# Attention scores of a half row: both bank waits ahead of the first of two matmuls

## The chip, the cores and the metric

The kernel runs on one core of one Trainium2 chip. The metric is the device time of one execution in microseconds (us); lower is better.

## The reference, cut to what matters

Three blocks follow each other: cross attention of 4 x 128 queries to 4 x 2048 keys with 16 heads and a bias, a gated recurrence with ternary weights and its gated MLP, and a mixture of 8 experts. The change touches the first alone:

```python
h = NUM_HEADS                       # 16, each 32 wide
q = _split_heads(query_antecedent @ Wq, h) * d_head ** (-0.5)
k = _split_heads(memory_antecedent @ Wk, h)
v = _split_heads(memory_antecedent @ Wv, h)
logits = jnp.einsum('bhqd,bhkd->bhqk', q, k) + bias
weights = jax.nn.softmax(logits, axis=-1)
x = jnp.einsum('bhqk,bhkd->bhqd', weights, v)
b, _, l, d = x.shape
x = x.transpose(0, 2, 1, 3).reshape(b, l, h * d)
return x @ Wo
```

with 4 batches, 128 queries and 2048 keys. The two blocks behind it are the gated recurrence (its state goes through a scan) and `_moe` with the best 2 of 8 experts.

## The kernel before, in words

Everything of the attention is written out by hand: each engine has one program in order, and the engines meet in counted semaphores. `pe`, `dve`, `act` are TensorE, VectorE, ScalarE. `x.made(key)` counts a semaphore up when an instruction is done, and `wait_ge(*x.at(key))` waits for that count.

A batch `b` has four quads of four heads each; quad `n` has the place `g = n % 4` in its batch. A row `j` of a quad is one head: 128 queries by 2048 keys. It is scored in four chunks `c` of 512 keys, one matmul each (L482), and each chunk fills one of the three PSUM banks of the ring `scores`. VectorE takes a chunk out of its bank, adds the bias, keeps a running maximum (`add_bias`, L712, followed by the instruction that reads the accumulator), and so counts `biased` and sets the bank free. ScalarE takes the exponential of a whole row (L894). TensorE turns the weights over through the identity (`turn_pair`, 8 transposes of two key tiles, L502), ScalarE (L902) or VectorE (L722) moves them out, and TensorE multiplies them with the values (`multiply_pair`, L517, 16 matmuls of 32 columns for a pair, the weights loaded as 128x32 tiles). The quad's sums are turned at L527 (`turn_sums`), copied by VectorE at L738, and the quad is closed by VectorE at L746 (`finish`), which waits for the quad's last product.

The order of TensorE around the change: a quad has eight slots, two for a row. Slot `i` scores half a row, that is two chunks, and then turns a pair of key tiles of the quad before; in every second slot it also multiplies two pairs. In the first quad of a batch (`g = 0`), and in two slots of the second, projections of values and keys (L429 to L431, L412 to L414) stand in place of the turning. When the fourth quad has been scored, a tail without scores turns and multiplies what is left (`TAIL`), and the projections of the next batch follow. Between a batch's scores and the next batch's lie some 90 us of projections.

With three banks and two chunks a slot, chunk number k of a batch's sequence waits until VectorE is done with chunk k-3. The first chunk of a slot thus waits for a bank that has long been free or nearly so, the second for a bank that VectorE frees one chunk later. After quads with `turn_sums` the sums take a turn of the ring too, so that for one chunk `sums_copied` stands in place of `biased`.

The waits of a matmul are carried out ahead of its weight load. The diff touches `score` (removed) and `score_slot`.

Of the kernel before, what the change touches and what calls it, by code (L numbers as in the profile page):

```python
# [27 lines left out]
CHUNK = 512  # L28
# [105 lines left out]
def perceiver_block(nc, a, out):  # L134
    with ExitStack() as life:
        def sb(name, shape, dt, stack=life):
            return stack.enter_context(nc.sbuf_tensor(name, shape, dt))
# [4 lines left out]
        def events(name, keys, by=1):  # L142
            return Events(sem(name), list(keys), by)

        psum = life.enter_context(nc.psum_tensor("psum", [P, 8, BANK], F32))
# [16 lines left out]
        def scalars(name):  # L162
# [31 lines left out]
        qstack = sb("qstack", [P, 2, QUAD, P], F32R, region_r)  # L194
# [8 lines left out]
        wq_sb, wk_sb, wv_sb, _, x_in, q_all, q_hi, q_lo = (view(s) for s in range(8))  # L203
# [19 lines left out]
        queries_in = [events(f"queries{i}_in", [n for n in quads if n % 2 == i], 16)  # L223
                      for i in range(2)]
# [9 lines left out]
        def in_ring(n, j):  # L234
            return n % DT >= 2 or n % DT == 1 and j == 0

        def ring_turn(n, j):
            return QUAD * (n % DT - 2) + j + 1 if n % DT >= 2 else 0
# [14 lines left out]
        def stack_in(n, j):  # L253
            return ring_in[ring_turn(n, j) % len(RING_PLACES)] if in_ring(n, j) else early_in[j]

        def stack_landed(n, j):
            return stack_in(n, j).at(n, j, 1)
# [30 lines left out]
        scored, biased = (events(name, [(n, j, c) for n in quads for j in range(QUAD) for c in range(UNITS)])  # L288
                          for name in ("scored", "biased"))
# [20 lines left out]
        scores, work = Ring((0, 1, 2)), Ring((3, 4, 5, 6))  # L310
# [35 lines left out]
        def stack_place(n, j):  # L346
            if in_ring(n, j):
                return RING_PLACES[ring_turn(n, j) % len(RING_PLACES)]
            return early_stack[:, (QUAD * (n - n % DT + 1) + EARLY_AT[n % DT][j]) % PS, :]
# [50 lines left out]
        def tensor_attention(pe):  # L400
# [70 lines left out]
                                       stop=(k == DT - 1))  # L471
                    mm.then_inc(*q_projected.made(g))

            def score(n, j, c):
                if j == 0 and c == 0:
                    pe.wait_ge(*queries_in[n % 2].at(n))
                if c == 0:
                    pe.wait_ge(*stack_landed(n, j))
                w, free = scores.take((n, j, c), biased.at(n, j, c))
                if free:  # L480
                    pe.wait_ge(*free)
                pe.matmul(psum[:, w, :], qstack[:, n % 2, j, :],  # L482
                          stack_place(n, j)[:, c * CHUNK:(c + 1) * CHUNK], start=True,
                          stop=True).then_inc(*scored.made(n, j, c))

            def score_slot(n, i):
                j, half = divmod(i, HALVES)
                for c in (2 * half, 2 * half + 1):
                    score(n, j, c)

            def turn_pair(n, p):
                w = pair_bank(p)
# [93 lines left out]
            for b in range(B):  # L586
# [13 lines left out]
                for n in range(DT * b, DT * (b + 1)):  # L600
                    for i in range(SLOTS_OF_QUAD):
                        score_slot(n, i)
                        project_beside(b, next(beside, ()))
                        step = step_of_slot(n, i)
                        if step is not None:
                            turn_and_weigh(b, step)
                        if n > DT * b and i == SUMS_AT:
                            turn_sums(n - 1)
# [2246 lines left out]
        @block.tensor  # L2855
        def _(engine):
            tail = tensor_attention(engine)
            tensor_recurrence(engine, *tail)
            tensor_experts(engine)
# [55 lines left out]
```

## Time and profile before

| | |
|---|---|
| median of 3 runs | 1005.64 us (1005.37 to 1005.93) |
| span of the profiled execution, first to last instruction | 1003.4 us |
| TensorE busy, weight loads busy | 970.8 us (97%), 815.7 us (81%) |
| VectorE, ScalarE, GpSimd busy | 599.4, 488.4, 258.3 us |
| granted TensorE clock, mean | 0.998 |

The profiled execution's span is 1003.4 us; the 2.2 us up to the median of the runs lie around it, before the first and after the last instruction. In the tables of the profile a load of weights (PEld) and its matmul (PE) are rows of their own; ends of matmuls are modelled, starts are not, so TensorE's pace is read from the starts of the loads.

### The profile page before, as it was taken

To read this page: it belongs to the slowest core of one execution; us is meant where nothing else is said; L and a number is where in the kernel's file an instruction comes from. 1 tells how busy PE (TensorE), PEld (TensorE's weight loads), DVE (VectorE), ACT (ScalarE), POOL (GpSimd) and SP (SyncE) were. 2 spreads that over 40 slices of the span, in tenths; PEclk is the share of its full clock that TensorE was granted. 3 is DMA by queue.
4 is the path that set the end of the run, shared out by engine and by line. 5 is a ranking of instruction groups with operands and counts; after the bars stand their busy time and mean duration, and the time that the engine had idled before them with its cause. 6 is when DMAs were issued, how large, how long until landed. Compare 5 with 4: busy or idle time off the path is not lost. (4 is left out here: it accounts for less than half of the span.)

```text
span 1003.4 us, 18226 instructions
## 1 busy us (share of the span) xinstructions
PE 970.8 (97%) x7342; PEld 815.7 (81%) x7350; DVE 599.4 (60%) x1178; ACT 488.4 (49%) x633; POOL 258.3 (26%) x254
## 2 busy tenths in 40 slices
PE   9999999999999999999999999987899999999996
PEld 8888788888778888788888787554589999999995
DVE  6517895565886467886364886685652112455552
ACT  4211885171886155787051687578621102455551
POOL 2202830002840001850000760678400201111100
PEclk9999999999999999999999999999999999999999
DMA  8294861524771615781421787400079949699930
GB/s 293 71 192 85 179 153 46 212 84 120 176 171 49 275 42 168 173 199 46 164 83 48 173 177 267 157 2 0 33 270 382 373 165 332 227 381 345 336 110 13
DMA packets 77597, 169.92 MB, mean 169 GB/s; under 512 B 6473, under 2 KB 17609, under 8 KB 72385
## 3 DMA queue, kind: packets, MB, share of 16 engines
q1 hardware_dynamic: 75392, 163.87, 53.2%
q0 software_dynamic: 2112, 4.80, 2.1%
q8 instruction: 60, 0.98, 0.4%
q14 instruction: 33, 0.26, 0.1%
HBM read 119.01 MB, written 16.10 MB: 135 GB/s over the span
## 5 line engine op out<-in xcount | busy, mean ns | idle before, releaser
L995 POOL CAST stack<-kT 128x2048 fp32r<-128x2048 f32 x32 | 62.8, 1976 | 381.4 <-ACT kT L850 374.0
L712 DVE CUSTOM_DVE_ANT_0 prob<-psum,biasmap,top 128x512 f32<-128x512 f32 x192 | 144.2, 751 | 15.5 <-PE psum L482 7.0
L894 ACT ACTIVATE prob<-prob,top 128x2048 f32<-128x2048 f32 x64 | 128.7, 2010 | 37.7 <-DVE top L712 37.7
L2319 PE MATMUL psum<-xT,wring 128*128 128x128 f32 (+3 forms) x1024 | 133.9, 291 | 0.4 <-ACT xT L2673 0.4
L502 PE MATMUL psum<-ident,prob 128*128 128x128 f32 x1024 | 130.8, 274 | 1.3 <-ACT probT L902 1.3
L2319 PEld LDWEIGHTS psum<-xT,wring 128*128 128x128 f32 x1024 | 130.4, 191 | 1.8 <-ACT xT L2673 0.7
L502 PEld LDWEIGHTS psum<-ident,prob 128*128 128x128 f32 x1024 | 116.7, 140 | 16.0 <-issue 4.4
L850 ACT COPY kT<-psum 128x512 f32<-128x512 f32 x64 | 37.5, 585 | 188.9 <-PE psum L414 188.7
L429 PE MATMUL psum<-wv_hi,ctx_part 128*128 128x512 f32 x256 | 99.9, 390 | 0.1
L431 PE MATMUL psum<-wv_hi,ctx_part 128*128 128x512 f32 x256 | 99.7, 389 | 0.0
L430 PE MATMUL psum<-wv_lo,ctx_part 128*128 128x512 f32 x256 | 99.6, 389 | 0.0
L412 PE MATMUL psum<-ctx_part,wk_hi 128*128 128x512 f32 x240 | 94.2, 392 | 0.0
L414 PE MATMUL psum<-ctx_part,wk_lo 128*128 128x512 f32 x240 | 93.4, 389 | 0.0
L413 PE MATMUL psum<-ctx_part,wk_hi 128*128 128x512 f32 x240 | 93.4, 389 | 0.0
L666 DVE COPY v<-psum 128x512 f32<-128x512 f32 x48 | 32.8, 688 | 78.4 <-PE psum L431 78.4
L902 ACT COPY probT<-psum 128x1024 f32<-128x1024 f32 x64 | 63.3, 1007 | 18.6 <-PE psum L502 18.6
L2784 POOL DMA_INDIRECT out_x<-y_rows,row_id x11 | 17.0, 1542 | 208.7 <-DVE y_rows L2582 94.9
L2555 DVE TENSOR_SCALAR hidden<-psum,b 128x128 f32<-128x128 f32 (+3 forms) x64 | 23.5, 367 | 74.5 <-PE psum L2319 74.3
L2686 ACT ACTIVATE hidden<-psum,b 128x128 f32<-128x128 f32 (+3 forms) x64 | 24.4, 381 | 76.6 <-PE psum L2319 74.8
L2561 DVE TENSOR_TENSOR w_low<-wring,w_high 128x1024 fp32r<-128x1024 f32 x40 | 48.0, 1220 | 22.8 <-ACT w_high L2695 22.8
L2334 PE MATMUL psum<-hidden,wring 128*128 128x192 f32 (+2 forms) x384 | 58.0, 313 | 0.0
L2334 PEld LDWEIGHTS psum<-hidden,wring 128*128 128x128 f32 x384 | 57.3, 190 | 0.1
(284 smaller groups left out, 1771.0 us busy)
## 6 DMA issues: line engine op xcount, KB each, us to landing
wring<-in_w SPq DMA_DIRECT2D x64, 1024.0 KB, 8.6
ctx_raw<-in_ctx_t SPq DMA_DIRECT2D x15, 1024.0 KB, 6.0
stack<-stack SPq DMA_DIRECT2D x32, 256.0 KB, 4.7
early_stack<-early_stack SPq DMA_DIRECT2D x28, 256.0 KB, 3.8
prob<-in_w_gate_t SPq DMA_DIRECT2D x1, 5632.0 KB, 17.5
stack<-key_stack SPq DMA_DIRECT2D x20, 256.0 KB, 4.0
query_stacks<-prob SPq DMA_DIRECT2D x16, 256.0 KB, 5.4
qstack<-query_stacks SPq DMA_DIRECT2D x16, 256.0 KB, 5.2
```

Of the source, the lines that this page charges most:

```text
L412: pe.matmul(psum[:, w, :], wh, ctx_part[:, half, 0, k, :], start=(k == 0), stop=False)
L413: pe.matmul(psum[:, w, :], wh, ctx_part[:, half, 1, k, :], start=False, stop=False)
L414: mm = pe.matmul(psum[:, w, :], wl, ctx_part[:, half, 0, k, :], start=False, stop=(k == DT - 1))
L429: pe.matmul(psum[:, w, :], ch, wv_hi[:, k, :], start=(k == 0), stop=False)
L430: pe.matmul(psum[:, w, :], ch, wv_lo[:, k, :], start=False, stop=False)
L431: mm = pe.matmul(psum[:, w, :], cl, wv_hi[:, k, :], start=False, stop=(k == DT - 1))
L502: mm = pe.transpose(psum[:, w + i, j * P:(j + 1) * P], prob[:, prob_slot(n, j), kt * P:(kt + 1) * P], ident[:, :])
L712: dve.tensor_tensor_reduce(prob[:, slot, keys], psum[:, scores.of[n, j, c], :], biasmap[:, keys], 1.0, top[:, h, (c + 1) % 2:(c + 1) % 2 + ...
L894: act.activation(prob[:, slot, :], prob[:, slot, :], ACT.Exp, bias=top[:, h, 1:2], scale=-1.0, accum_out=top[:, h, 2:3]).then_inc(*raised. ...
L902: act.copy(turned_pair(n, p), psum[:, w:w + 2, :].rearrange("p i (j q) -> p i j q", j=QUAD)).then_inc(*moved_a.made(n, p))
L2319: mm = pe.matmul(psum[:, w, 0:width], wring[piece][:, k, h % 4 * P:(h % 4 + 1) * P], xT[:, q % 2, k, 0:width], start=(k == 0), stop=(k == ...
L2334: mm = pe.matmul(y_place(q, k), wring[piece][:, h % 4, k * P:(k + 1) * P], hidden[:, h, 0:width], start=(h == 0), stop=(h == HT - 1))
```

## The change

The matmuls, their operands, their banks and their order stay. For each of the 128 half rows, the waits of the second chunk's bank are moved ahead of the first chunk's matmul. The first matmul then starts when both banks are free; the second has no wait of its own.

```diff
-            def score(n, j, c):
-                if j == 0 and c == 0:
-                    pe.wait_ge(*queries_in[n % 2].at(n))
-                if c == 0:
-                    pe.wait_ge(*stack_landed(n, j))
-                w, free = scores.take((n, j, c), biased.at(n, j, c))
-                if free:
-                    pe.wait_ge(*free)
-                pe.matmul(psum[:, w, :], qstack[:, n % 2, j, :],
-                          stack_place(n, j)[:, c * CHUNK:(c + 1) * CHUNK], start=True,
-                          stop=True).then_inc(*scored.made(n, j, c))
-
             def score_slot(n, i):
                 j, half = divmod(i, HALVES)
-                for c in (2 * half, 2 * half + 1):
-                    score(n, j, c)
+                chunks = (2 * half, 2 * half + 1)
+                if i == 0:
+                    pe.wait_ge(*queries_in[n % 2].at(n))
+                if half == 0:
+                    pe.wait_ge(*stack_landed(n, j))
+                places = [scores.take((n, j, c), biased.at(n, j, c)) for c in chunks]
+                for _, free in places:
+                    if free:
+                        pe.wait_ge(*free)
+                for c, (w, _) in zip(chunks, places):
+                    pe.matmul(psum[:, w, :], qstack[:, n % 2, j, :],
+                              stack_place(n, j)[:, c * CHUNK:(c + 1) * CHUNK], start=True,
+                              stop=True).then_inc(*scored.made(n, j, c))
```

TensorE's order in the second row of the third quad of batch 0, before: the two chunks of each slot (L482), then the transposes (L502). In brackets are the semaphores that stand ahead of an instruction; x2 means twice the same.

```order
L482 MATMUL psum<-stack,qstack 128x512 [waits biased,stack2_in]
L482 MATMUL psum<-stack,qstack 128x512 [waits biased]
L502 MATMUL psum<-ident,prob 128x128 [waits moved_a,raised]
L502 MATMUL psum<-ident,prob 128x128 x7
L482 MATMUL psum<-stack,qstack 128x512 [waits biased] x2
L502 MATMUL psum<-ident,prob 128x128 [waits moved_v]
```

The same place after the change (the lines are L486 and L501 there):

```order
L486 MATMUL psum<-stack,qstack 128x512 [waits biased,stack2_in]
L486 MATMUL psum<-stack,qstack 128x512
L501 MATMUL psum<-ident,prob 128x128 [waits moved_a,raised]
L501 MATMUL psum<-ident,prob 128x128 x7
L486 MATMUL psum<-stack,qstack 128x512 [waits biased]
L486 MATMUL psum<-stack,qstack 128x512
L501 MATMUL psum<-ident,prob 128x128 [waits moved_v]
```

Each second chunk has lost its wait; the first has its own and the second's, which the listing names once. No instruction that computes has moved.

The last row of the same quad on TensorE, before, where the quad's sums (L527) have taken a turn of the ring:

```order
L527 MATMUL psum<-ident,inverse 128x128 [waits biased,spread_out]
L482 MATMUL psum<-key_stack,qstack 128x512 [waits biased,stack4_in]
L482 MATMUL psum<-key_stack,qstack 128x512 [waits biased]
L502 MATMUL psum<-ident,prob 128x128 [waits moved_a]
L502 MATMUL psum<-ident,prob 128x128 x7
L482 MATMUL psum<-key_stack,qstack 128x512 [waits sums_copied]
L482 MATMUL psum<-key_stack,qstack 128x512 [waits biased]
```

And after:

```order
L526 MATMUL psum<-ident,inverse 128x128 [waits biased,spread_out]
L486 MATMUL psum<-key_stack,qstack 128x512 [waits biased,stack4_in]
L486 MATMUL psum<-key_stack,qstack 128x512
L501 MATMUL psum<-ident,prob 128x128 [waits moved_a]
L501 MATMUL psum<-ident,prob 128x128 x7
L486 MATMUL psum<-key_stack,qstack 128x512 [waits biased,sums_copied]
L486 MATMUL psum<-key_stack,qstack 128x512
```

## Rows read from the trace of the kernel before

**Rows 1.** The page: busy us, share of the span, instructions.

```profile
PE 970.8 (97%) x7342; PEld 815.7 (81%) x7350; DVE 599.4 (60%) x1178; ACT 488.4 (49%) x633; POOL 258.3 (26%) x254
```

**Rows 2.** Windows (us, then busy PE, PEld, DVE, ACT, POOL; clock): quads 1, 3, projections.

```profile
110.20:122.90 12.70, 11.77 (x124) 9.16 (x126) 11.99 (x33) 11.42 (x14) 12.53 (x6) 1.00 0.74 165
...
139.20:155.50 16.30, 16.14 (x217) 13.13 (x213) 14.70 (x39) 13.88 (x15) 0.00 (x0) 1.00 0.20 70
155.50:246.40 90.90, 90.90 (x616) 75.52 (x609) 48.90 (x48) 33.41 (x33) 2.43 (x1) 1.00 0.34 116
```

**Rows 3.** Waits of the weight loads: whole span, quad 1, quad 3 (us, times, longest).

```profile
PEld psum L482 <- DVE top L712: 13.0, 29, 0.8
...
PEld psum L482 <- DVE top L712: 1.5, 3, 0.8
...
PEld psum L482 <- DVE top L712: 0.8, 2, 0.4
```

**Rows 4.** Timeline of the weight loads, quad 3, row 1: two slots.

```profile
143.32 0.30 PEld L482 LDWEIGHTS psum<-stack,qstack 128*128 128x128 f32 x2 [0.20 <-issue]
143.66 1.02 PEld L502 LDWEIGHTS psum<-ident,prob 128*128 128x128 f32 x8
144.66 0.19 PEld L482 LDWEIGHTS psum<-stack,qstack 128*128 128x128 f32 x1
145.25 0.19 PEld L482 LDWEIGHTS psum<-stack,qstack 128*128 128x128 f32 x1 [0.40 <-DVE top L712]
145.38 0.14 PEld L502 LDWEIGHTS psum<-ident,prob 128*128 128x128 f32 x1
```

**Rows 5.** Timeline of VectorE beside it.

```profile
145.11 0.08 DVE L712 DVE_READ_ACCUMULATOR2_ANT top<- 128x1 f32 x1
145.23 0.75 DVE L712 CUSTOM_DVE_ANT_0 prob<-psum,biasmap,top 128x512 f32<-128x512 f32 x1
```

**Rows 6.** Timelines, quad 1: weight loads and VectorE where two waits stand ahead.

```profile
110.55 0.19 PEld L482 LDWEIGHTS psum<-early_stack,qstack 128*128 128x128 f32 x1
...
110.36 0.08 DVE L712 DVE_READ_ACCUMULATOR2_ANT top<- 128x1 f32 x1
111.44 0.08 DVE L712 DVE_READ_ACCUMULATOR2_ANT top<- 128x1 f32 x1
112.23 0.68 DVE L712 CUSTOM_DVE_ANT_0 prob<-psum,biasmap 128x512 f32<-128x512 f32 x1
```

**Rows 7.** Timelines, start of quad 3: first chunk's loads, VectorE's first chunk.

```profile
139.44 0.30 PEld L482 LDWEIGHTS psum<-stack,qstack 128*128 128x128 f32 x2 [0.20 <-issue]
...
140.09 0.69 DVE L712 CUSTOM_DVE_ANT_0 prob<-psum,biasmap 128x512 f32<-128x512 f32 x1 [0.63 <-PE psum L482]
```

**Rows 8.** Timeline of VectorE where quad 2 is closed.

```profile
147.81 0.29 DVE L746 TENSOR_TENSOR oT<-psum,inverse 128x128 f32<-128x128 f32 x1 [0.23 <-PE psum L517]
```

**Rows 9.** Timeline of the weight loads, last slot of quad 3.

```profile
153.43 0.19 PEld L482 LDWEIGHTS psum<-stack,qstack 128*128 128x128 f32 x1 [0.39 <-DVE top L712]
```

**Rows 10.** Chain that ended last, behind the last scores of batch 3.

```profile
612.87 0.50 PE psum L482
613.37 0.87 PE psum L502 x8
...
631.46 3.45 PE psum L542 x8
634.93 0.70 DVE x L783
```

**Rows 11.** Weight loads, batch 2, quad 0: slot 1, where VectorE is late.

```profile
402.27 0.19 PEld L482 LDWEIGHTS psum<-early_stack,qstack 128*128 128x128 f32 x1 [0.60 <-DVE top L712]
402.38 0.19 PEld L429 LDWEIGHTS psum<-wv_hi,ctx_part 128*128 128x128 f32 x1
```

**Rows 12.** Weight loads: the first pair of all (its second carries no wait), and one whose second does.

```profile
93.68 0.41 PEld L482 LDWEIGHTS psum<-early_stack,qstack 128*128 128x128 f32 x2
...
100.93 0.41 PEld L482 LDWEIGHTS psum<-early_stack,qstack 128*128 128x128 f32 x2
```

## The prediction

> **What bounds the kernel now.** I read the page first: TensorE is busy 97% of the span [rows 1], so whatever lengthens its program lengthens the kernel unless an idle stretch takes it up. The windows by stage say where such stretches are. In the projections behind the scores it is busy 90.90 of 90.90 us; nothing is taken up there. In quad 3 (the last of a batch) it is busy 16.14 of 16.30 us, with VectorE at 14.70 beside it; in quad 1 VectorE is the bound, busy 11.99 of 12.70 us [rows 2]. The change can only act where scores are made, so I then asked for the waits of the weight loads. Over the span the loads of L482 sat idle 13.0 us behind VectorE's L712, in 29 places: 3 in quad 1, 2 in quad 3 (quad 2 has 2 as well), which is 7 a batch and 28 in four, and one more [rows 3]. The timeline tells which of the two chunks waits. In slot 3 of quad 3 the first chunk's load starts at 144.66, at once behind the transposes; the second's starts at 145.25, after 0.40 idle, and the transposes' load follows at 145.38 [rows 4]. VectorE finished the accumulator of the decisive chunk at 145.11 + 0.08 = 145.19 [rows 5]. So TensorE uses part of the wait to make the first chunk, and that work is what the change puts behind the wait.
>
> **The change at one waiting half row.** Count from the moment VectorE frees the second bank to the moment TensorE is loading for what comes next.
>
> Before: 145.38 - 145.19 = 0.19 us [rows 4, 5]. It holds the reaction to the semaphore (145.25 - 145.19 = 0.06) and one chunk's share, 0.13.
>
> After: the reaction, then both chunks. For the two chunks the slot ahead is the measure, one that waits for no bank: 143.66 - 143.32 = 0.34 us from its first load to the next work's [rows 4]. For the reaction, the decisive wait now stands ahead of a matmul with a wait of its own, so it is a wait instruction and not part of the load. Quad 1 has that form: the accumulator is read at 110.36 + 0.08 = 110.44 and the load, with two waits ahead, starts at 110.55, 0.11 us later [rows 6]. That makes 0.11 + 0.34 = 0.45 us.
>
> Difference: 0.45 - 0.19 = 0.26, with unrounded starts nearer to 0.28. I take **0.27 us** for each waiting half row whose delay is not taken up. Its bounds: 0.21, if the wait instruction costs no more than the wait on the load (0.34 + 0.06 - 0.19), and 0.34, if the pair after an empty queue were as wide as in the projections (0.41, [rows 12]).
>
> **How many of the 28 count.** A delay of TensorE is taken up by the next wait for VectorE, if VectorE itself has not moved. So I followed who waits for whom.
>
> In quad 1 VectorE works without a gap, so its times stay; each of the three waits absorbs the delay of the one before, and what leaves the quad is one delay, that of its last slot. In quads 2 and 3 VectorE does wait for TensorE, twice in each. Its first chunk of the quad starts after 0.63 us idle, released by the scores loaded at 139.44 [rows 7], and the closing of the quad before starts at 147.81 after 0.23 idle, released by L517 [rows 8]. At each of these the delay of TensorE passes to VectorE in full, because VectorE was idle for it. The first lies between the last slot of a quad and slot 3 of the next, the second between slot 3 and the last slot (whose wait is 0.39 again, [rows 9]). So the delays of slot 3 and slot 7 add: two in quad 2, two in quad 3. Behind the last one come the tail and the projections, which have no slack [rows 2]; in batch 3 the chain that ended last runs from that score through the transposes, products and L542 to VectorE at 634.93, all on TensorE [rows 10].
>
> One and two and two: 5 a batch, 20 in all, 20 x 0.27 = **5.4 us**.
>
> The 29th place is in batch 2, where VectorE is late in the first quad. There the second load starts at 402.27 and the next at 402.38 [rows 11]; with the release 0.05 before the load, the next would come at 402.22 + 0.45 = 402.67, 0.3 us later, and projections follow. This adds **0.3 us**. The slots in which both banks come free before or just about when the first chunk is due, over a hundred, cost nothing: their wait instructions run while earlier matmuls are still going. Where it comes a trifle late (slots 1 and 5 of quads 2 and 3) TensorE loses a little in that slot, and the long wait of slot 3 or 7 takes it back; the closing of the quad, between them, waits for a product of slot 3.
>
> **What VectorE loses.** Scores now start later, so is VectorE still fed? After the release it has one chunk in hand: 0.04 us until it starts, then 0.75, and the accumulator's 0.08 partly behind that [rows 5], so that it wants the next 0.79 to 0.87 after the release. The late chunk's load starts 0.11 after the release, and 139.44 to 140.09 shows 0.65 us from a load to VectorE's start [rows 7]: 0.76, which leaves 0.03 to 0.11, in the middle 0.07. That is thin, but enough. In quad 1's even slots the chunk in hand is a row's last and VectorE goes on after 112.23 - 111.52 = 0.71 us [rows 6], so up to 0.05 can be lost there, at most 0.6 us in all; I take none.
>
> **What the second chunk gains.** Nothing that a row shows. In the first pair of all the second chunk carries no wait, in that of 100.93 it does; both pairs of loads take 0.41 us [rows 12].
>
> [...]
>
> **The sum.** 1003.4 + 5.4 + 0.3 = 1009.1 us of span. With the 2.2 us that lie around it, 1011.3; against the median, 1005.64 + 5.7 = 1011.3, since the profiled execution stands to the median as the span does. I say **1011.3 us**, 0.6% slower.
>
> **Rivals.**
> *The delays are absorbed.* If VectorE's two places a quad had other causes (the 0.63 us also ends with a product of TensorE that frees the row's buffer, and 0.23 is short), only the last slot of each batch would cost: 4 x 0.27 + 0.3 = 1.4 us, 1007.0, no change to speak of. If only the closing is slack, 3 a batch: 3.5 us, 1009.1. For it: waits of VectorE are what a bank ring is there to hide. Against it: both are put down to TensorE, and they repeat in every quad.
> *VectorE starves.* If that 0.07 us isn't there, say because the start of a matmul after an empty queue is later by 0.1, then each of the 20, and the two even ones of quad 1, would cost up to 0.1 more: 2 to 2.5 us, 1013.6.
> *Faster.* A second load without a wait lies wholly under the first's matmul. Now it starts 0.30 - 0.19 = 0.11 us behind it [rows 4]. If that went away in all 128 pairs, 14 us would go, 5.7 come: 997.3. It decides from 0.05 us a pair on. [...]
>
> **Chances and range.** My forecast with its neighbours (12 to 22 delays that add, 0.21 to 0.34 each) 0.75; absorbed 0.11; starved 0.10; faster 0.04. The range runs from the absorbed case, 1007.0, to the starved one, 1013.6; some 0.12 lie outside. A measurement of this kernel tells about 0.2%, or 2.0 us, from no change. Slower by that much: forecast and starved, and a little of absorbed, 0.87. Within: 0.09. Faster: 0.04.
>
> **What the profile of after would show.** In slot 3 and slot 7 of quads 2 and 3 one idle stretch ahead of the first chunk's load, none inside the pair; 0.45 us from the end of VectorE's accumulator to the transposes' load, where 0.19 was. Quad 3, 16.30 us long before [rows 2], is up by 0.54, and quad 2 too; quad 1 is up by 0.27. Quads of all batches grow alike, projections not. VectorE's idle time behind TensorE stays as it is. I am wrong if quads 2 and 3 grow by less than 0.3 (absorbed), if VectorE shows new gaps between chunks of a row (starved), or if pairs without a wait take under 0.34 us (faster).

## The result and the profile after

The changed kernel takes 1013.14 us (median of 4 runs, 1012.42 to 1015.18) against 1005.5; the ratio is 1.0081 (95% interval 1.0068 to 1.0094), and 1.0076 (1.0063 to 1.0090) when it was timed again. It is slower, as forecast, but by 7.6 to 8.1 us where I had worked out 5.7. 1005.5 times 1.0081 is 1013.6, the far edge of the range and the time that I had given to the rival in which VectorE starves; the profile shows below that this rival's mechanism is absent. The profiled execution has a span of 1010.6 us, 7.2 more than before.

The weight loads of quad 3 of batch 0 after the change, row 1 (the place of [rows 4]), then its last slot (the place of [rows 9]):

```profile
144.88 0.30 PEld L486 LDWEIGHTS psum<-stack,qstack 128*128 128x128 f32 x2 [0.20 <-issue]
145.23 1.02 PEld L501 LDWEIGHTS psum<-ident,prob 128*128 128x128 f32 x8
146.75 0.30 PEld L486 LDWEIGHTS psum<-stack,qstack 128*128 128x128 f32 x2 [0.50 <-DVE top L711]
147.10 0.37 PEld L501 LDWEIGHTS psum<-ident,prob 128*128 128x128 f32 x2
...
155.22 0.30 PEld L486 LDWEIGHTS psum<-stack,qstack 128*128 128x128 f32 x2 [0.35 <-issue]
```

VectorE beside it, from the start of the quad to the closing of the quad before:

```profile
141.53 0.69 DVE L711 CUSTOM_DVE_ANT_0 prob<-psum,biasmap 128x512 f32<-128x512 f32 x1 [0.92 <-PE psum L486]
...
146.55 0.09 DVE L711 DVE_READ_ACCUMULATOR2_ANT top<- 128x1 f32 x1
146.68 0.75 DVE L711 CUSTOM_DVE_ANT_0 prob<-psum,biasmap,top 128x512 f32<-128x512 f32 x1
...
147.47 0.75 DVE L711 CUSTOM_DVE_ANT_0 prob<-psum,biasmap,top 128x512 f32<-128x512 f32 x1
...
149.54 0.29 DVE L745 TENSOR_TENSOR oT<-psum,inverse 128x128 f32<-128x128 f32 x1 [0.51 <-PE psum L516]
```

The two loads of a waiting pair are now one row, with the whole wait ahead of them. From the accumulator's end (146.64) to the transposes' load (147.10) it is 0.46 us, where [rows 4, 5] gave 0.19. VectorE goes on at its old pace of 0.79 us a chunk, so it doesn't starve. It waits longer for TensorE at exactly the two places of [rows 7, 8]: 0.92 for 0.63, and 0.51 for 0.23, each 0.28 to 0.29 more. That is the delay on its way from one engine to the other.

The growth of each quad, from the starts of TensorE's loads: from the load behind the last pair of scores of one quad to the load behind the last pair of the next. Quad 0 thus includes the projections ahead of it; in batch 0 it is counted from the first scores.

```
growth, us           quad 0   quad 1   quad 2   quad 3   four batches
forecast               0*      0.27     0.54     0.54     5.4 + 0.3*
after, batch 0        0.11     0.27     0.59     0.58
after, batch 1        0.02     0.28     0.59     0.58
after, batch 2        0.66     0.27     0.59     0.57
after, batch 3        0.02     0.29     0.60     0.61     6.6
profiled once more, batch 2 and sum
                      0.62     0.28     0.60     0.57     6.6
* the 0.3 in batch 2's quad 0
```

The 20 delays are there, 0.29 us each on average. But quad 0 of batch 2 has twice what I gave it. Its first scores are where there had been no wait at all. First the kernel before, then the changed one:

```profile
399.67 0.41 PEld L482 LDWEIGHTS psum<-early_stack,qstack 128*128 128x128 f32 x2
```

```profile
404.33 0.30 PEld L486 LDWEIGHTS psum<-early_stack,qstack 128*128 128x128 f32 x2 [1.22 <-issue]
404.67 0.19 PEld L429 LDWEIGHTS psum<-wv_hi,ctx_part 128*128 128x128 f32 x1
```

In front of the quads there is another difference: the first scores come 0.45 us later, from a delay at the kernel's first weights.

### The profile page after: what moved, and what is told of

Same layout as the page of the kernel before. It is cut to its first block and busy times, and to the rows that moved or that the text cites. A ratio compares the mean times of both kernels' runs of the same rounds, so it can differ in the third digit from the quotient of the medians.

```text
span 1010.6 us, 18312 instructions
## 1 busy us (share of the span) xinstructions
PE 974.9 (96%) x7350; PEld 816.0 (81%) x7350; DVE 599.7 (59%) x1178; ACT 488.0 (48%) x633; POOL 259.4 (26%) x254
## 5 line engine op out<-in xcount | busy, mean ns | idle before, releaser
L501 PEld LDWEIGHTS psum<-ident,prob 128*128 128x128 f32 x1024 | 116.7, 140 | 17.7 <-issue 4.4
L501 PE MATMUL psum<-ident,prob 128*128 128x128 f32 x1024 | 130.8, 274 | 0.2
```

What stands on the lines that cost most here:

```text
L501: mm = pe.transpose(psum[:, w + i, j * P:(j + 1) * P], prob[:, prob_slot(n, j), kt * P:(kt + 1) * P], ident[:, :])
```

## The experiments

All ratios are to the kernel before on the same chip. Edits are shown against the changed kernel unless said otherwise.

### Both kernels again

> The kernel before, once more. Theory A (the 1.1 us of the new span beyond the attention are chance of DMA landings, 0.45 at the first weights and 0.65 at the start of batch 2): these two places vary between executions of this same kernel too, by some tenths to 1 us; ratio 1.000. Theory B (they belong to the change): the first loads of batch 0 and the start of batch 2 stand within 0.05 us of the profile before.

> The changed kernel, once more. Both theories: quads 1, 2, 3 of each batch grow by 0.28, 0.58, 0.58 us as in its first profile, 5.8 us in all. Theory A: span of 1009.2 to 1011, ratio 1.006 to 1.008, with other values at the first weights and at batch 2. Theory B: the same 0.45 and 0.65 us again, 7.2 us, ratio 1.0075.

Before again: 0.9997 (0.9988 to 1.0006). After again: 1.0076. By the load of the first scores the four profiles stand at 0, 0.36 (before), 0.45 and -0.13 us (after), so that difference is chance and theory A holds there. At batch 2 the kernel before repeats to 0.01 us and the changed kernel to 0.04 (0.66, 0.62): there theory B holds. So neither theory is right for both. A third thing differs between executions: in the windows of 720 to 740 us, behind the attention, the granted clock (last but two) was 1.00 in the first profile of before and 0.83 in the second:

```profile
720.00:740.00 20.00, 17.18 (x136) 14.45 (x134) 14.18 (x55) 5.20 (x11) 1.48 (x4) 1.00 0.36 123
```

```profile
720.00:740.00 20.00, 18.89 (x134) 16.87 (x132) 13.16 (x50) 5.10 (x11) 1.48 (x4) 0.83 0.27 94
```

By the starts of its loads the second lost 1.1 us there. Both kernels have such executions, with a mean clock down to 0.992. This is why the trace of one execution can't be set against a median to better than about 1 us here.

### The twenty alone, and all but the twenty

```diff
                 places = [scores.take((n, j, c), biased.at(n, j, c)) for c in chunks]
-                for _, free in places:
+                ahead = (n % DT == 1 and i == 7 or n % DT >= 2 and i in (3, 7))
+                for _, free in places[:HALVES if ahead else 1]:
                     if free:
                         pe.wait_ge(*free)
-                for c, (w, _) in zip(chunks, places):
+                for at, (c, (w, free)) in enumerate(zip(chunks, places)):
+                    if at and free and not ahead:
+                        pe.wait_ge(*free)
                     pe.matmul(
```

The second kernel has `not` ahead of the condition.

> The change in 20 of 128 half rows alone: slot 7 of quad 1, slots 3 and 7 of quads 2 and 3 of each batch. Theory (delays of these 20 add, all others are absorbed or cost nothing): 20 x 0.29 = 5.8 us, ratio 1.0058, the same growth of each quad as with the whole change. Rival (every one of the some 50 half rows that find VectorE late gives a share): 2 to 4 us.

> The change in the other 108 half rows, and not in those 20. Theory: each delay is taken up by the next wait for VectorE, nothing is left: 0 to 0.4 us, ratio 0.9995 to 1.0005. Rival (each gives a share): 2 to 4 us, ratio 1.002 to 1.004.

The twenty: 1.0069 (1.0055 to 1.0083), quads 1 to 3 of batch 0 grow by 0.28, 0.58, 0.59, the other batches alike, quad 0 of batch 2 by 0.02; 5.8 us in sum, as in the changed kernel. All but the twenty: 1.0011 (1.0001 to 1.0020), quads 1 to 3 within 0.02 of zero in every batch, but 0.09 in the first quad of batch 0 and 0.58 in that of batch 2. That is 0.7 us, more than the 0 to 0.4 of my theory and far from the rival's 2 to 4. The 20 places are the right ones, and what the other 108 cost lies in quad 0, not in the waits for VectorE of the later quads.

### Slot 3 alone, slot 7 alone

The same edit with `n % DT >= 2 and i == 3`, and with `n % DT >= 1 and i == 7`.

> The change in slot 3 of quads 2 and 3 alone, 8 half rows. Theory (the delay passes to VectorE where it closes the quad behind, and so to slot 7 and beyond): 0.29 us in each of quads 2 and 3, 0 in quad 1, 2.3 us, ratio 1.0023. Rival (slot 7's wait takes it up): 0.

> The change in slot 7 of quads 1, 2 and 3 alone, 12 half rows. Theory (the delay passes to VectorE at the first chunk of the next quad): 0.29 us in each of the three quads, 3.5 us, ratio 1.0035. Rival (the wait of the next quad's slot 3 takes it up, and only the last of a batch counts): 0.29 in quad 3 alone, 1.2 us, ratio 1.001.

Slot 3: quads 1 to 3 grow by -0.01, 0.29, 0.30 in batch 0, 2.4 us in all (ratio 1.0036, 1.0023 to 1.0049). Slot 7: 0.28, 0.29, 0.30, 3.5 us (1.0032, 1.0021 to 1.0043). Each alone passes in full through the place at which VectorE waits for TensorE; the rival, that the next wait takes the delay up, is refuted for both. 2.4 and 3.5 make the 5.8 of the twenty.

These traces also show what the local sum had left out. From the wait to the first load of the transposes the delay is 0.27 us, as worked out; between the first and the second load of the transposes 0.02 more are lost, in each of the five places of batch 0, and stay.

### Where the decisive wait sits

One kernel leaves out the first bank's wait where it is covered, the other writes the two waits in the other order:

```diff
-                for _, free in places:
-                    if free:
-                        pe.wait_ge(*free)
+                frees = [free for _, free in places if free]
+                if len(frees) == 2 and frees[0][0] is frees[1][0]:
+                    frees = frees[1:]
+                for free in frees:
+                    pe.wait_ge(*free)
```

```diff
-                for _, free in places:
+                for _, free in reversed(places):
```

> The changed kernel, with the first bank's wait left out where the second's later count of the same semaphore covers it, so that the decisive wait sits on the load itself and not in an instruction ahead of it. Theory (0.06 to 0.07 us of each of the 20 delays of 0.29 is the wait instruction): quads 1, 2, 3 grow by 0.22, 0.44, 0.44 us, 4.4 us in four batches, and 0.3 in batch 2's first quad with its instruction load where it was before: 4.7 to 5 us, ratio 1.005. Rival (the instruction costs nothing, the delay is the chunk alone): 0.28, 0.58, 0.58 again, 5.8 us.

> The changed kernel with the two waits written in the other order: as many wait instructions (78 more than before), but in odd slots the decisive count sits on the load and the old one in the instruction ahead. Theory (it matters where the decisive wait sits, and the number of instructions moves the instruction loading): quads 1, 2, 3 grow by 0.22, 0.44, 0.44 us as with one wait, and the first quad of batch 2 by 0.6 as in the changed kernel: 5.1 us, ratio 1.005. Rival (each wait instruction costs, wherever the decisive one is): 0.28, 0.58, 0.58.

With one wait: 0.27, 0.53, 0.52 in batch 0 (ratio 1.0060, 1.0045 to 1.0074), between the two theories. The starts say why: in slot 3 the load comes 0.04 us behind the semaphore (which counts 0.01 us after the accumulator's end), in slot 7 still 0.10, because there the first bank is freed by `sums_copied`, another semaphore, so that two waits stayed and the decisive one in the instruction ahead. I had overlooked that. The second kernel clears it up: 0.21, 0.46, 0.47 in batch 0 (1.0059, 1.0045 to 1.0073), with as many wait instructions as the changed kernel. Its slot 3 of quad 3, weight loads and VectorE:

```profile
145.91 0.30 PEld L486 LDWEIGHTS psum<-stack,qstack 128*128 128x128 f32 x2 [0.51 <-DVE top L711]
146.25 0.37 PEld L501 LDWEIGHTS psum<-ident,prob 128*128 128x128 f32 x2
```

```profile
145.78 0.08 DVE L711 DVE_READ_ACCUMULATOR2_ANT top<- 128x1 f32 x1
```

From 145.86 to 145.91 it is 0.05, where the changed kernel has 146.64 to 146.75, 0.11. So of 0.29 us a delay, 0.06 is the wait instruction in which the decisive count sits; a wait instruction with an old count costs nothing at its own place (here one stands ahead of the decisive wait in all 20 places, and the load comes 0.05 behind the accumulator as in the kernel before). The pair itself is 0.34 in every version.

The kernel with one wait shows one thing more. Its first scores of batch 2 come in time (0.02 us late), and there quad 0 grows by 0.31 us, all in slot 1: the 0.3 us of my forecast, by its mechanism. In the changed kernel this cost doesn't show, because TensorE comes late to that slot.

### The wait instructions without the change

Against the kernel before, in `score`:

```diff
                 if free:
                     pe.wait_ge(*free)
+                if c == 2 and (n, j) != (0, 0) or (j, c) == (0, 0) and n:
+                    pe.wait_ge(*keys_copied.at(0, 0, 0))
                 pe.matmul(
```

> The kernel before, with 78 more wait instructions on TensorE at the places where the changed kernel has its 78, each for a count that was reached long ago; the waits for banks stay where they were. Theory (the 0.6 us at the start of batch 2 come from the place of TensorE's instruction loading, which the longer program moves onto the landing of that batch's first key stack): 0.6 us at the first quad of batch 2 and 0 in all other quads, an instruction load of 16384 bytes in the 5 us ahead of the first score there, ratio 1.0006. Rival (the 0.6 us come from the moved wait of slot 1 there): nothing anywhere, ratio 1.0000.

Ratio 1.0009 (1.0000 to 1.0017). All quads stand within 0.02 us of before, but quad 0 of batch 2 is longer by 0.77:

```profile
401.47 0.30 PEld L484 LDWEIGHTS psum<-early_stack,qstack 128*128 128x128 f32 x2 [1.35 <-issue]
```

The key stack of those scores on its way, with the us from issue to landing last in the line: the transfer issued at 395.69 in the kernel before, then that issued at 396.19 in this one:

```profile
early_stack<-early_stack SPq DMA_DIRECT2D x1, 256.0 KB, 3.7
```

```profile
early_stack<-early_stack SPq DMA_DIRECT2D x1, 256.0 KB, 5.2
```

The queues of this kernel from 395 to 402 us have a load of instructions:

```profile
q8 instruction: 1, 0.02, 1.2%
```

The key stack takes 5.2 us to land, not 3.7. No wait for a bank was moved, and the wait added right ahead of batches 1 and 3 costs nothing there; what is left of the change is the length of TensorE's program. The profiles divide cleanly. Five, of the four kernels with 58 to 78 added wait instructions (the changed kernel twice, all but the twenty, the decisive wait on the load, this one), have the instruction load 3.9 to 4.0 us ahead of the first score, and that score 1.1 to 1.3 us late, 0.06 us behind the landing of its key stack. The nine with 0 to 20 added have the instruction load 1.9 to 6.0 us behind that score, and the stack landed 0.2 to 0.3 us ahead of it. (Among these nine the place also varies between two profiles of the kernel before: 1.9 and 6.0.) 0.43 of the delay is given back one slot later, where TensorE had waited 0.60 us for VectorE ([rows 11]) and now doesn't.

### The other way round

If the first chunk inside the wait was worth 0.23 us, more work inside should be worth more. These two keep the kernel before, and put the second chunk behind the transposes, in the twenty half rows and in all 44 odd slots with transposes:

```diff
-                        score_slot(n, i)
-                        project_beside(b, next(beside, ()))
                         step = step_of_slot(n, i)
-                        if step is not None:
-                            turn_and_weigh(b, step)
+                        if n % DT == 1 and i == 7 or n % DT >= 2 and i in (3, 7):
+                            j, half = divmod(i, HALVES)
+                            score(n, j, 2 * half)
+                            turn_pair(*pair_of_step(b, step))
+                            score(n, j, 2 * half + 1)
+                            for weighed in weighed_behind(step):
+                                multiply_pair(*pair_of_step(b, weighed))
+                        else:
+                            score_slot(n, i)
+                            project_beside(b, next(beside, ()))
+                            if step is not None:
+                                turn_and_weigh(b, step)
```

> The other way round: in the 20 half rows whose second chunk waits long, that chunk stands behind the pair of transposes that follows (first chunk, 8 transposes, second chunk, products); all else as before. Theory (in these 20 TensorE loses 0.38 us each to a wait that the 0.87 us of transposes cover, and VectorE wants the late chunk only after its chunk in hand): 0.38 us less in quad 1 and 0.76 less in quads 2 and 3 of each batch, 7.6 us, ratio 0.9925. Rival (VectorE is the bound there and the wait turns up elsewhere): 0 to 2 us less.

> As the one with twenty, but in all odd slots that have transposes (slots 1, 3, 5, 7 of quads 2 and 3, slots 3, 5, 7 of quad 1), 44 half rows. Theory (the short waits of slots 1 and 5 are 0.01 us each, those inside quad 1 only move since VectorE is the bound there): as with twenty, within 0.1%. Rival (the transposes behind a short wait delay the second chunk and so VectorE): slower than with twenty by 0.1 to 0.5%.

The twenty: 1000.21 us, ratio 0.9942 (0.9929 to 0.9956). All odd slots: 0.9946 (0.9932 to 0.9959), the same. Both beat the kernel before, by 5.4 to 5.8 us where I had 7.6. In slot 3 of quad 3:

```profile
143.73 0.19 PEld L482 LDWEIGHTS psum<-stack,qstack 128*128 128x128 f32 x1
143.86 1.01 PEld L502 LDWEIGHTS psum<-ident,prob 128*128 128x128 f32 x8
144.84 0.19 PEld L482 LDWEIGHTS psum<-stack,qstack 128*128 128x128 f32 x1
145.27 0.38 PEld L517 LDWEIGHTS psum<-prob,v 128*32 128x32 f32 x16 [0.25 <-issue]
```

There is no wait for VectorE in this slot any more. But the products' first load now idles 0.25 us behind the chunk, so I tried the chunk in the middle of the transposes (`turn_pair` calls it after the first four).

> In the 20 half rows whose second chunk waits long, that chunk stands between the fourth and the fifth of the 8 transposes, not behind the eighth; all else as before. Theory (behind the transposes it stood ahead of the products, whose first load then came 0.13 us later because of the long matmul before it; between them it is covered all the same, since the wait it avoids is 0.4 us and four transposes are 0.44): ratio 0.992 to 0.9935, 6.5 to 8 us less than before. Rival (VectorE, busy 15.1 of 16.2 us in quad 3 with the chunk behind, is the bound by now): as with the chunk behind, 0.994, 5.7 us less.

999.71 us, ratio 0.9941 (0.9927 to 0.9955): no better than behind them, as the rival had said, but not for its reason. The same slot with the chunk between:

```profile
144.59 0.19 PEld L482 LDWEIGHTS psum<-stack,qstack 128*128 128x128 f32 x1
...
146.14 0.81 PEld L519 LDWEIGHTS psum<-prob,v 128*32 128x32 f32 x32 [0.17 <-issue]
```

From the first chunk's load to the products' first load it is 1.55 us, and 1.54 with the chunk behind the transposes. Both hold within 0.02 us in all twenty places, and neither has a wait inside. So TensorE needs the same time for either order, and the 0.25 us was no loss that an order could win back. Before the change these stretches took 1.84 to 1.92 us; together they are 7.0 us shorter with the chunk behind. One us of this is lost again in a new wait, once in quad 2 of each batch (0.23 to 0.25 us each). In the kernel with the chunk behind, quad 2 of batch 0:

```profile
PEld psum L482 <- DVE top L720: 0.2, 1, 0.2
```

From the first scores of one quad to those of the next, quads 1 shrink by 0.36 to 0.38 us, quads 2 by 0.45 to 0.57 and, up to the same load of the tail, quads 3 by 0.67 to 0.69 there, 6.2 us in all, where I had 0.38, 0.76 and 0.76. So the rival's mechanism, a wait for VectorE that turns up elsewhere, is real in quad 2 alone. In quad 3 TensorE waits for VectorE nowhere, and VectorE still has one idle place behind TensorE, here with the chunk between:

```profile
DVE prob L722 <- PE psum L482: 0.3, 1, 0.3
```

## Where the prediction was right, and the step that failed

*The first chunk's work falls behind the wait.* Right: 0.46 us from release to next work where I had 0.45. *The price of one delay.* 0.29 for 0.27, inside its bounds: the sum was right up to the first load of the transposes, and the 0.02 behind it were missing. 20 times that is 0.4 us too little. *Twenty of the 28 add.* Right, shown by the twenty alone (5.8 us) and the rest (0 in quads 1 to 3), and split by slots 3 and 7. That VectorE works without a gap in quad 1 was not quite so: it waits for TensorE 0.26 and 0.32 us there, but both ahead of TensorE's three waits. *VectorE is fed.* Right: no new gap between the chunks of a row, so that the starved rival is refuted although its time was met. *The second chunk gains nothing.* Right: a pair without a wait takes 0.34 us as in [rows 4], and in the projections 0.45 to the next load as before. No second load came earlier because its wait was gone: in the 128 pairs of the changed kernel it starts 0.11 (78), 0.17 (12) or 0.23 us (38) behind the first, the same three distances as in the kernel before where neither load of a pair is held up. It lies under the first's matmul in all 128, and the 0.11 us of the rival *Faster* stayed.

**The step that failed** is the term for batch 2's quad 0, and the sentence that wait instructions in the slots without a late bank "cost nothing". I gave 0.3 us to that quad, by a mechanism of slot 1. It measured 0.62 to 0.66, by another one in slot 0; mine is real (0.31 us in the kernel with one wait), but hidden in the changed kernel. With the 78 wait instructions TensorE's program is longer, a load of instructions stands ahead of batch 2's first score and not behind it, and the key stack takes 1.3 to 1.5 us longer to land. I had counted the 78 and taken each for free, which it is at its own place. I also left out 0.1 us of slot 1 in batch 0. Repeatable in the traces are 5.8 + 0.65 + 0.1 = 6.6 us where I had 5.7, of which this step is 0.35, the delays' 0.02 us are 0.4 and slot 1 is 0.1.

Between these 6.6 and the 7.6 to 8.1 of the ratios 1.0 to 1.5 us stay open; that is more than what the failed step explains, and no quad shows it. The intervals of the two ratios reach down to 6.8 and 6.3 us, and single executions differ by as much (0.45 at the first weights, 1.1 where the clock fell). The ratios of the twenty alone (6.9) and of slot 3 alone (3.6) also lie about 1 us above their traces (5.8 and 2.4), that of slot 7 alone (3.2 for 3.5) doesn't. The clock is a small part at most: among the executions with a mean granted clock of 0.998 the median spans are 1011.0 us (4 of the changed kernel) and 1003.6 (38 of the kernel before), still 7.4 apart.

One sign that I had listed was wrong: VectorE's idle time behind TensorE did not stay, it grew by 0.28 at both places. It had to, since its work was the same in a longer quad.

That the longer program costs these 0.65 us is shown by the added waits alone. That it does so through the instruction load is inferred from their standing together in all 14 profiles. Which transfer holds up which wasn't taken apart.

## What to carry to other kernels

Work that an engine can do before a wait belongs before it: gathering waits at the head of a group costs the group's first members where the last wait is long (here 0.29 us in each of 20 places, of which 0.23 is the first chunk's work), and the trace says where that is (an idle stretch between two of the group's loads). A delay counts in full if the engine waited for is itself idle behind the waiter somewhere in the cycle (VectorE was, for 0.63 and 0.23 us, and then for 0.92 and 0.51); look for that place before calling a delay absorbed. And count instructions as well as waits: 58 to 78 more in one engine's program came with an instruction load beside a transfer that something was waiting for, and 0.6 to 0.8 us.

## What the hardware showed beyond that

With the decisive count in a wait instruction of its own (the changed kernel) the load behind it started 0.10 us after the semaphore, with it on the load itself (the waits in the other order) 0.04. Behind the 128x512 matmul of a chunk (the twenty with the second chunk behind the transposes) the first 32-column load of the products came after 0.24 to 0.25 us idle (20 places), where behind the 128x128 transposes it was 0.17 (60 places of the kernel before).
